# Edge-network message passing on one core: TensorE's products of a half in two parts, with a gathered tile between them

## The reference

```python
w = relu(edgefeats @ fnet_w1 + fnet_b1) @ fnet_w2 + fnet_b2      # per edge, 16 x 16
W = w.reshape(-1, nc, nc)
for _ in range(2):
    xj  = hx[edge_src]                                            # gather, one row per edge
    m   = einsum('ei,eio->eo', xj, W)                             # message
    agg = segment_sum(m, edge_dst) * inv_deg[:, None]
    hx  = gru_cell(agg, hx)
return layernorm(x + hx)
```

## Time and profile before

| | us |
|---|---|
| median of 3 runs | 6714.77 (6712.53 to 6716.03) |
| span of the profiled execution | 6694.6 |
| PE busy in it | 5648.0 (84%) |
| DVE busy | 4296.9 (64%) |
| ACT busy | 3179.0 (47%) |
| POOL busy | 3811.1 (57%) |

### The profile page before, as it was taken

How to read it: one execution, slowest core, us unless ns; L and a number is a source line. 1 busy time by engine, 2 the same in 40 slices (tenths; PEclk the granted TensorE clock), 3 DMA queues, 4 the chain that set the end, 5 groups by cost and what they waited for, 6 DMA issues and landing times.

```text
span 6694.6 us, 119595 instructions
## 1 busy us (share of the span) xinstructions
PE 5648.0 (84%) x38360; PEld 4666.6 (70%) x38361; DVE 4296.9 (64%) x7146; ACT 3179.0 (47%) x5259; POOL 3811.1 (57%) x4021
## 2 busy tenths in 40 slices
PE   2888888888888888888858888888888888888887
PEld 1777777777777777777647777776777777777775
DVE  3766666666666666666636666666666666666665
ACT  1554555445554545454325454454545454444442
POOL 6355555555555555555555555555555555555553
PEclk7988998889898999998878898898988889888887
DMA  4111111111111111111111111111111111111110
GB/s 107 46 34 48 34 48 34 48 34 48 34 48 44 39 48 34 48 34 48 25 47 29 40 29 40 33 37 39 31 40 29 40 29 41 29 40 29 40 29 20
DMA packets 197656, 263.32 MB, mean 39 GB/s; under 512 B 95745, under 2 KB 165942, under 8 KB 184205
## 3 DMA queue, kind: packets, MB, share of 16 engines
q1 hardware_dynamic: 61885, 216.66, 9.5%
q0 software_dynamic: 128192, 33.07, 4.8%
q10 hardware_dynamic: 7026, 6.21, 0.4%
HBM read 195.73 MB, written 54.92 MB: 37 GB/s over the span
## 4 chain that ended last, share of the span: by engine, by line
PE 65%; issue 14%; another core or an unknown queue 10%; ACT 6%; DVE 3%; DVEq 1%; DMA 0%; POOL 0%; ACTq 0%; POOLq 0%; SPq 0%
PE ps_all L722 45%; PE ps_all L732 8%; ACT src_hot L603 3%; PE ps_all L755 3%; PE ps_all L745 3%; PE ps_all L709 3%; PE ps_all L776 2%; ACT src_hot L607 2%; DVE shared L1137 1%; DVE fan L1092 1%; PE ps_all L762 0%; ACT shared L576 0%; ACT h_sb L570 0%; DVE xg L1145 0%
## 5 line engine op out<-in xcount | busy, mean ns | idle before, releaser
L722 PE MATMUL ps_all<-parts,src_hot 125*128 125x400 f32 x18048 | 3820.4, 368 | 258.7 <-issue 166.4
L722 PEld LDWEIGHTS ps_all<-parts,src_hot 125*128 125x128 f32 x18048 | 3501.9, 202 | 482.6 <-issue 367.7
L535 POOL DMA_INDIRECT xg<-in_x,idx x2027 | 1923.4, 949 | 1394.3 <-issue 556.1
L535 POOL DMA_INDIRECT xg<-h_rows,idx x1979 | 1873.1, 946 | 1371.6 <-issue 518.7
L1137 DVE TENSOR_TENSOR shared<-ps_all,at_hot 128x400 f32<-128x400 f32 x2256 | 1211.8, 566 | 1858.8 <-remote 1168.4
L603 ACT ACTIVATE src_hot<-keys,neg_key 128x384 fp32r<-128x384 int16 (+1 forms) x3072 | 1617.0, 599 | 1653.1 <-remote 979.0
L732 PE MATMUL ps_all<-fan,h_sb 128*32 128x160 f32 x12544 | 825.0, 316 | 489.5 <-issue 435.8
L1092 DVE TENSOR_TENSOR fan<-xg,ps_all 128x1280 f32<-128x1280 f32 x784 | 1158.8, 1478 | 88.0 <-DVE xg L1145 33.4
L607 ACT ACTIVATE src_hot<-src_hot 128x1536 fp32r<-128x1536 f32 (+1 forms) x768 | 1122.2, 1461 | 72.3 <-ACT src_hot L603 2.8
L1145 DVE TENSOR_REDUCE xg<-shared 128x48 f32<-128x1200 f32 (+1 forms) x768 | 1056.7, 1376 | 75.6 <-DVE shared L1137 1.0
L732 PEld LDWEIGHTS ps_all<-fan,h_sb 128*32 128x32 f32 x12544 | 391.8, 111 | 842.4 <-issue 794.9
(11 more groups left out here) (120 smaller groups left out, 1383.7 us busy)
## 6 DMA issues: line engine op xcount, KB each, us to landing
keys<-key_d SPq DMA_DIRECT2D x96, 768.0 KB
h_d<-h_sb SPq DMA_DIRECT2D x49, 1056.0 KB
h_sb<-h_d SPq DMA_DIRECT2D x49, 1056.0 KB
xg<-in_x,idx POOLq DMA_INDIRECT x2027
xg<-h_rows,idx POOLq DMA_INDIRECT x1979
ef<-in_ef_t SPq DMA_DIRECT2D x49, 420.0 KB
acc_all<-agg_t SPq DMA_DIRECT2D x1, 3161.0 KB
idx<-in_src_tiles SPq DMA_DIRECT2D x98, 32.0 KB
```

What stands on the lines that cost most here:

```text
L535: pool.indirect_dma_start(out=xg[:, buf, at, 0:C], out_offset=None, in_=rows_of, in_offset=bass.IndirectOffsetOnAxis(ap=idx[:, buf, at:at ...
L722: last = pe.matmul(ps_g[j], src_hot[0:KP, k % 2, kb, j * P:(j + 1) * P], parts[0:KP, m, kb, :], start=(kb == 0 and m == 0), stop=(kb == KB ...
```

## The change

`products` is called twice in each half, once per four tiles (`u`). The first call keeps both waits, the second one raises `s_p`. Between the two calls the half's first gathered tile (`j = 0`) runs; its other tiles (`j = 1, 2`) stay at the end of the half. The wait for `s_parts` moves with the first tile. No instruction is added or left out; those of one tile are moved.

```diff
-            def gather_rows(rnd, s, k):
+            def gather_rows(rnd, s, k, js):
                 for j, (n, _, _) in enumerate(pe_tiles(rnd, k)):
-                    pe.wait_ge(s_src_hot, pe_count(rnd, s, n) + 1)
...
+                    if j in js:
+                        pe.wait_ge(s_src_hot, pe_count(rnd, s, n) + 1)
...
-            def products(sup, buf, k):
-                pe.wait_ge(s_fan, sup * HPS + k + 1)
-                wait_pos(pe, s_pev, sup * HPS + k - 1)
-                for u in range(2):
-                    for b in range(BPS):
+            def products(sup, buf, k, u):
+                if u == 0:
+                    pe.wait_ge(s_fan, sup * HPS + k + 1)
+                    wait_pos(pe, s_pev, sup * HPS + k - 1)
+                for b in range(BPS):
...
-                last.then_inc(s_p, 1)
+                if u == 1:
+                    last.then_inc(s_p, 1)
...
                     for k in range(HPS):
-                        products(sup, buf, k)
+                        products(sup, buf, k, 0)
+                        if not is_last(i):
+                            if is_first(i, par) and k == 0:
+                                pe.wait_ge(s_parts, rnd + 1)
+                            gather_rows(rnd, s + 1, k, (0,))
+                        products(sup, buf, k, 1)
...
                         if not is_last(i):
-                            if is_first(i, par) and k == 0:
-                                pe.wait_ge(s_parts, rnd + 1)
-                            gather_rows(rnd, s + 1, k)
+                            gather_rows(rnd, s + 1, k, (1, 2))
```

More of the change, by code:

```diff
@@ L726, in products @@
-            def products(sup, buf, k):
-                pe.wait_ge(s_fan, sup * HPS + k + 1)
-                wait_pos(pe, s_pev, sup * HPS + k - 1)
-                for u in range(2):
-                    for b in range(BPS):
[L732 to L735, removed]
-                last.then_inc(s_p, 1)
+                    if j in js:
+                        pe.wait_ge(s_src_hot, pe_count(rnd, s, n) + 1)
+                        if isinstance(s, int) and s == 1 and slot_free(rnd, k, j) < 0:
+                            wait_pos(pe, s_picked, pe_total(rnd))
+                        else:
+                            pe.wait_ge(s_picked, pe_count(rnd, s, slot_free(rnd, k, j)) + 1)
+                        for kb in range(KB):
+                            for m in range(PARTS):
+                                last = pe.matmul(ps_g[j], src_hot[0:KP, k % 2, kb, j * P:(j + 1) * P],
+                                                 parts[0:KP, m, kb, :],
+                                                 start=(kb == 0 and m == 0), stop=(kb == KB - 1 and m == PARTS - 1))
+                        last.then_inc(s_g, 1)
@@ new lines, in products @@
+            def products(sup, buf, k, u):
[3 more added lines that the diff above has]
+                for b in range(BPS):
+                    last = pe.matmul(
+                        ps_p[k % 2][b * HID:(b + 1) * HID, u * C * WIN:(u + 1) * C * WIN],
+                        h_sb[:, buf, k * HT + u * BPS + b, 0:HID],
+                        fan[:, k % 2, u * BPS + b].rearrange("p i n -> p (i n)"), start=True, stop=True)
+                if u == 1:
+                    last.then_inc(s_p, 1)
```

## The result

The changed kernel takes 6747.77 us (median of 14 runs, 6732.52 to 6768.64), the kernel before 6710.32 in the same job (14 runs): ratio 1.0058, interval 1.0044 to 1.0071. It is 0.6% slower where 0.9% faster was predicted. A "stall" is here what the prediction read at 2091: PE's matmuls come out in drops of a few, and no semaphore holds them. In some jobs both kernels ran without such stalls and took some 20% less time. The ratios are always against the kernel before in the same job, and each result says "with stalls" or "without stalls". Two single runs lie far off their series, 9502.77 us (nops, clock 1.0) and 6697.83 us (more signals, clock 0.653, where every run with stalls has 0.870 to 0.926); they are in no ratio, have no trace and are not explained.

What follows compares the result with a forecast made beforehand. PE was taken to bound the kernel, held to its average pace by stalls and half-speed clock. Added 253 + 221 + 144 = 618 us, more than given back by fewer stalls, net -58 us: 6655 us, range 6430 to 6970.

Steps and rivals of the forecast that it cites:

- The switches: PE entering and leaving the products twice: 0.33 us per half, 253 us in all, ends 0 and 0.5 us.
- The one-hots: First tile's waits for ACT's one-hot: 221 us added in half 1, 144 us in half 0.
- The row "over 300": Sign of being right: PE idle ahead of L722 for ACT's L607 up from 74 us to over 300.
- DVE's bank: First tile's wait for DVE's pick: taken as 0, upper end 0.5 us in two halves of eight, 96 us.
- What comes back: PE's stall loss falls with the record surplus, 12.1 to 5.1 us per super; net 65.7 to 65.1, -58 us.
- The signs I had named for "right": Two 8-record product stretches per half, one-hot wait over 300, products' idle below 489.5, clock above 0.882, 13.9 records per us.
- A: Clock falls at half 1's new wait, slowing the gather: 2.7 us in each super, 259 us, 6915; chance 0.28.
- B: PE's stalls have another cause and keep their number: 7333, or 6968 with only the switches added; chance 0.14.
- C: PE's records per us are all that counts and none is added: 6715, within 0.2%; chance 0.10.
- D: Stalls at the products go, loss perhaps a quarter: -2.7 us per super, 6455; chance 0.12.

Runs made afterwards that it cites:

- nops: Kernel before with 8 empty TensorE instructions ahead of each half's gather, 6144 in all: 0.9979 of the kernel before with stalls.
- more signals: Kernel before with four more semaphore increments per gathered tile, 9024 in all, for which nobody waits: 0.9999 of the kernel before without stalls.
- both early: Changed kernel, half 1's one-hot made ahead of the aggregate's copy and first tile's pick ahead of window sums: 0.9863 with stalls, 1.0362 and 1.0364 without.
- small matmuls: Kernel before with four tiny matmuls ahead of each half's products, results unread: 1.0143 of the kernel before without stalls, 1.0021 with stalls.
- tile ahead: Changed kernel, but the half's first gathered tile runs ahead of whole, unsplit products: 1.0524 of the kernel before without stalls, 1.02 with stalls.
- third tile: Changed kernel, with the half before's third tile between the product parts instead of this half's first: 1.0097 with stalls, 1.051 without.
- the early one-hot in the kernel before: Kernel before with ACT making half 1's one-hot ahead of the copy of the aggregate: 0.9969 with stalls, 0.9999 without.

## Why the prediction was wrong

**The switches: right.** 0.33 us per half, 253 us. Without stalls nothing hides them: both early costs 187 us over the kernel before. The switches make 253 of it and the one-hot 27 more (34.9 - 8.2). Less are `fan` with 59 (127.2 - 68.0), the pick with 11 (19.8 - 9.0) and the clock with 13 (0.983 to 0.986). The sum is 197.

**The one-hots: right.** 365 us added were expected, and 358 came (436.5 - 78.9), or 279 by the waits' rows (353.4 - 74.4). Half 1 has 266.0 us where 74 + 221 were taken, half 0 has 170.5 where 144 were. The row "over 300" is met. Without stalls it is 184 (192.0 - 8.2). In half 0 the wait is there when the hand-over is late, as taken.

**DVE's bank: the term that failed.** "I take 0, upper end 0.5 in two halves of eight (96 us)". It is 326 us (367.4 - 41.7), or 157 by the rows (168.4 - 11.0). I had read that the tile was "just covered, with 0.2 us to spare" from one half with signals on time, though I had myself read a late hand-over the earlier trace rows and used it for the one-hot. The same lateness makes DVE's window sum late, and the pick is queued behind it. The upper end was too low too. That lateness is the cause is shown by the pair of traces: 5.7 us and the wait, 0.22 us and none.

**What comes back: the step that failed for the sign.** I took it that stalls follow the surplus of records over the average pace. By this law a super is shorter than before whatever is added to it, up to some 12 us: the stalls give back more than is put in. Even the 921 us that were added in truth, 9.6 us per super, would give by it 53.6 + 9.6 + 12.1 x 0.47 / 2.7 = 65.3 us (0.47 is 783 / 63.2 - 11.92), 0.4 less than before, and a time near 6680. So the bank's term alone does not explain why the sign was wrong; the law does. The small matmuls refute it, 13.6 records per us in the same time. What the kernels with stalls show instead is only that time in which PE waits takes the stalls' place:

| kernel, all with stalls | added, us | span or ratio says | came back | stalls |
|---|---|---|---|---|
| before | 0 | 0 | 0 | 179 |
| both early | 253 + 116 - 9 - 11 = 349 | -92 | 441 | 124 |
| tile ahead | 471 + 454 - 20 = 905 | +134 | 771 | 55 |
| changed | 253 + 358 + 326 - 16 = 921 | +72 | 849 | 58 |
| changed, second chip | 253 + 393 + 400 - 8 = 1038 | +102 | 936 | 48 |
| third tile | 253 + 75 + 16 + 703 = 1047 | +66 | 981 | 42 |

(Added: switches, one-hot, pick and `fan`, the waits sorted as above and less 78.9, 41.7 and 36.6; tile ahead changes no switch between products and gather. The third column is the difference of the spans for the changed kernel, else the ratio's difference times the time before. The kernels come from different jobs, so it is good to some tens of us.) With 349 us added, more came back than was put in; with 900 and more, less, some 0.85 to 0.94 of it. Where the 849 us of the changed kernel came from can be summed from the records. PE's idle time outside the three sorted waits fell by 554 (868 to 314); the clock's rise is (0.118 x 6694.6 - 0.094 x 6766.7) = 154; the rest, some 140, is left over, most of it in PE's busy time, since the matmuls of a stall count as busy (busy fell by 36 although the switches add 253).

Without the pick's 326 us the change would have added some 600. No kernel lies there; between 349 and 905 the table would put it about even with the kernel before. That is argued from the table; no run took away the pick's wait alone where there were stalls.

The signs I had named for "right" were all met: two stretches of products in a half, the one-hot above 300 us, 149.0 us idle ahead of the products, clock 0.906, 84 records in the 6.02 us from 2045.98, 14.0 per us where 13.9 were named. The time went the other way, because none of them looked at the pick, nor at what comes back.

**The rivals.** A was half right. I counted the first tile's time by the wait ahead of it: over 4 us, 55 of 56 tiles ran over 2.4 us instead of 1.66; from 2 to 4 us, 46 of 124; below, 11 of 588. Of these 112 only 23 are in half 1, 24% of the 96 supers where A wanted 22%, and 52 are in half 5. Each costs some 1.3 us (2.97 - 1.66), 147 us in all. But half-speed time as a whole fell, from some 1580 us to 0.188 x 6766.7 = 1272, as the stalls took more of it with them. B is wrong with stalls (58 of 179 are left) and right without: nothing can come back, and the change costs 396 us, 7.7%. C falls by the result, 0.6% where it allowed 0.2%, and by the small matmuls. D did not come: the stalls at the products went (435.8 to 104.8 us), but into waits.

**What I could not know** from one trace is that the kernel has the two conditions. In both the change loses, by 0.6 to 1.5% and by 7.7%. Both early wins 1.4% with stalls and loses 3.6% without; no version beat the kernel before in both. Of the versions run in both, the early one-hot in the kernel before is the only one slower in neither (0.9969 and 0.9999).

**Open:** what makes the stalls. It is not the chip, the kernel, the sequencer's instructions, the number of matmuls and weight loads, or the bursts in the products. Other work on the same chip was neither seen nor excluded. The loading of instructions was not tested either: the queues that do it moved the same 5.70 and 1.68 MB with stalls and without. That signals come late and that PE stalls go together in every trace, but which causes which was not shown.

## What to carry to other kernels

Where an order puts a consumer closer to its producer, price the hand-over at its worst in the trace, not at its best, for every engine whose signal it uses: the same late signal that I allowed ACT I forgot for DVE. Idle time for no semaphore can take up most of an added wait, here 0.85 to 0.94 of it, and give back as much of a removed one, so the sum of waits alone tells neither sign nor size. A law that gives back more than is put in needs a test of its own before a forecast stands on it: adding work that does nothing is a cheap one. And before a change is judged by under 2%, time the kernel before in several jobs: here it has two times, 5145 and 6710 us, and they disagree on which version is best.

## What the runs showed of the hardware that I had not expected

- TensorE's stream can stall for some 7 us every 37 us in this kernel, or hardly at all: 179 stalls and clock 0.881, or 3 and 0.983, on one chip and with the same work, 6710 against 5145 us.
- In the traces with stalls its signals come late: a median of 2.1 us from the end of the products to `s_p` in the kernel before, over 4.2 in one of ten; 0.04 us in both cases without stalls.
- Without stalls, waits of TensorE can cost more than their length: 157 us of them cost 211, and 53 of the other 54 are the clock, 0.977 against 0.986.
- 8 nops per half and 12,544 additional small records are hidden where there are stalls (0.9979, 1.0021). Where there are none the records cost 1.4%.
